# Causal attention on one core: masks taken off TensorE, small steps taken off VectorE

## The reference

```python
# 16 heads of 8 dimensions, 2 sequences of 2048, in chunks of 64 queries
scores = jnp.einsum('bhqd,bhkd->bhqk', qc, k) * scale
causal_mask = k_pos[None, :] > q_pos[:, None]
scores = jnp.where(causal_mask[None, None], -jnp.inf, scores)
m = jnp.max(scores, axis=-1, keepdims=True)
m = jnp.where(jnp.isinf(m), jnp.zeros_like(m), m)
p = jax.nn.softmax(scores - m, axis=-1)
oc = jnp.einsum('bhqk,bhkd->bhqd', p, v)
```

## Time and profile before

| | |
|---|---|
| median of three runs | 1788.74 us |
| profiled execution | 1792.63 us |
| its span | 1790.9 us |
| busy, TensorE / VectorE / ScalarE / GpSimd | 86% / 77% / 53% / 34% |
| L599, maxima: busy, idle before | 695.2 us, 64.8 us |
| L646, exponentials: busy, idle before | 607.1 us, 176.7 us |
| L687 and L695, masks: busy | 113.7 us, 115.3 us |

### The profile page before, as it was taken

How to read it: one execution, slowest core, us unless ns; L and a number is a source line. 1 busy time by engine, 2 the same in 40 slices (tenths; PEclk the granted TensorE clock), 3 DMA queues, 4 the chain that set the end, 5 groups by cost and what they waited for, 6 DMA issues and landing times. The chain is left out here.

```text
span 1790.9 us, 42250 instructions
## 1 busy us (share of the span) xinstructions
PE 1547.5 (86%) x13730; PEld 1004.8 (56%) x13730; DVE 1382.2 (77%) x2613; ACT 956.4 (53%) x2331; POOL 607.1 (34%) x416
## 2 busy tenths in 40 slices
PE   4499998999999999999972984899999999996376
PEld 3233333333333333333352874899999999996265
DVE  6799998998998999899653334588888888886522
ACT  4258887887887788788831322344444444442121
POOL 4600000000000000000015240988888888871633
PEclk9679999999999999999986996899999999997588
DMA  3320110011100110011063303011111222215340
GB/s 110 107 66 30 32 32 26 25 32 33 32 21 30 32 32 25 25 32 32 14 191 100 105 26 100 13 48 47 47 47 47 47 47 47 47 35 157 121 119 25
DMA packets 89477, 97.80 MB, mean 55 GB/s; under 512 B 12557, under 2 KB 74122, under 8 KB 89297
## 3 DMA queue, kind: packets, MB, share of 16 engines
q1 hardware_dynamic: 84176, 83.27, 16.4%
q0 software_dynamic: 5120, 12.26, 2.0%
HBM read 40.91 MB, written 31.85 MB: 41 GB/s over the span
## 5 line engine op out<-in xcount | busy, mean ns | idle before, releaser
L599 DVE TENSOR_REDUCE chunk_max<-ps_max 128x1 f32<-128x512 f32 (+3 forms) x1280 | 695.2, 604 | 64.8 <-PE ps_max L695 54.8
L646 ACT ACTIVATE probs<-ps_s 128x512 f32<-128x512 f32 (+3 forms) x1280 | 607.1, 534 | 176.7 <-PE ps_s L687 149.1
L1484 POOL TENSOR_TENSOR lane_products<-L,q 128x1024 f32<-128x1024 f32 x176 | 411.5, 2375 | 119.5 <-POOLq L1290 48.8
L668 PE MATMUL ps_s<-Qs,Ks 50*128 50x512 bf16 (+3 forms) x1280 | 376.7, 354 | 32.8 <-issue 13.8
L678 PE MATMUL ps_max<-Ks,Qs 48*128 48x512 bf16 (+3 forms) x1280 | 385.7, 360 | 13.8 <-POOL Vp L535 10.2
L741 PE MATMUL ps_o<-probs,Vp 128*32 128x512 f32 (+3 forms) x2560 | 344.1, 563 | 3.4 <-ACT probs L646 0.4
L668 PEld LDWEIGHTS ps_s<-Qs,Ks 50*128 50x128 bf16 x1280 | 113.9, 93 | 386.0 <-DVE chunk_max L599 327.1
L563 POOL COPY Vp<-V 128x128 f32 (+1 forms) x32 | 9.5, 299 | 740.3 <-PE ps_o L741 740.3
L1537 DVE TENSOR_TENSOR weighted<-exp_scores,psV_s 128x2048 f32<-128x2048 f32 x88 | 197.0, 2280 | 0.0
L1630 PE MATMUL psZT<-ident,weighted 128*128 128x128 f32 x1408 | 167.2, 274 | 1.8 <-DVE weighted L1537 1.8
L1630 PEld LDWEIGHTS psZT<-ident,weighted 128*128 128x128 f32 x1408 | 158.0, 141 | 2.0 <-DVE weighted L1537 2.0
(11 more groups left out here) (212 smaller groups left out, 2131.4 us busy)
## 6 DMA issues: line engine op xcount, KB each, us to landing
m_w<-in_L_ffn_w_dram SPq DMA_DIRECT2D x24, 512.0 KB, 6.9
dispatched<-blank SPq DMA_DIRECT2D x32, 258.0 KB, 3.0
m_d<-dispatched SPq DMA_DIRECT2D x14, 516.0 KB
L<-q SPq DMA_DIRECT2D x16, 448.0 KB
Qs<-q_parts SPq DMA_DIRECT2D x192, 32.0 KB
Ks<-k_parts SPq DMA_DIRECT2D x192, 32.0 KB
L<-q SPq DMA_DIRECT2D x20, 192.0 KB
L<-q SPq DMA_DIRECT2D x28, 128.0 KB
```

The source lines that it names most:

```text
L599: nc.vector.tensor_reduce(out, scores[:, 0:w], axis=AX.X, op=ALU.max).then_inc(max_reduced, 1)
L646: nc.scalar.activation(dst, ps_s[(k + r) % R][:, q0:], ACT.Exp, scale=SCALE).then_inc(exp_done, 1)
L668: last = nc.tensor.matmul(ps_s[(k + r) % R][:, q0:], K[r][rows, kt * P:(kt + 1) * P], Q[r][rows, g * QW + q0:(g + 1) * QW], start=True, st ...
L1484: return nc.gpsimd.tensor_tensor(out[:, l].rearrange("p (j m) d -> p j m d", m=LA), c.L[ch][:, :, l * LW:(l + 1) * LW].unsqueeze(2).broadc ...
```

## The change

The masks leave TensorE on both sides.

- For the maxima, VectorE uses `tensor_tensor_reduce` on the diagonal steps: it adds a constant fp32 tile `later` (0 at a query's own and earlier keys, -1e30 at later ones), writes the sum back to PSUM, and gives the maximum as an accumulated output. That instruction carries no wait of its own. Where the step before is a plain reduce, that reduce waits for the scores of both steps; where it is diagonal too (and at step 0), the wait stands on an increment of a counter ahead of it.
- For the exponentials, nothing is masked before them; GpSimd sets the later keys to zero in `probs` with `affine_select` on 128x128, 16 times a section, and `products` waits for the masks of its batch as well.
- Splitting the negated maximum in bf16 parts moves to GpSimd, at two places in its queue: after the masks of batches 0 to 2, and at the end of the section.
- ScalarE copies the combined output to SBUF after step 18 (`take_combined`), VectorE takes the reciprocal after step 22 (`invert`), GpSimd multiplies (`normalise`), after the masks of batches 3 to 5.
- The constants change: one tile `later` in place of the four bf16 mask tiles, and a zero tile for the split.

```diff
+    TAKE, INVERT = 18, 22
+    DIAGONAL = [kt >= 4 * g for g, kt in STEPS]
+    MASKS = [sum(DIAGONAL[:4 * n + 4]) for n in range(NBATCH)]
...
+            def split_maxima(s, r, f):
+                half = neg_max_b[r][:, f]
+                pool.wait_ge(neg_max_done, s * 2 + (f + 1))
+                nc.gpsimd.tensor_tensor(half[:, 0, :], neg_max[r][:, f, :], no_max[:], ALU.add).then_inc(neg_max_split, 1)
+                pool.wait_ge(neg_max_split, s * 4 + (2 * f + 1))
+                nc.gpsimd.tensor_tensor(half[:, 1, :], neg_max[r][:, f, :], half[:, 0, :], ALU.subtract)\
+                  .then_inc(neg_max_split, 1)
+
+            def normalise(s, p):
+
+                pool.wait_ge(inv_done, s)
+                nc.gpsimd.tensor_tensor(c.A_out[:, :, bass.ds(s - 1, 1), :].rearrange("p i s d -> p i (s d)"),
+                                        raw[p][:, :, 0:HD], inv[p][:].unsqueeze(2).broadcast_to([P, NQ, HD]), ALU.mult)\
+                  .then_inc(normalised, 1)
+
+            def mask(s, batches):
+                for n in batches:
+                    for q in range(4):
+                        k = 4 * n + q
+                        if DIAGONAL[k]:
+                            g, kt = STEPS[k]
+                            block = (probs[:, n % 3 * 4 + q] if n else probs0[:, q])[:, (kt - 4 * g) * P:(kt - 4 * g + 1) * P]
+                            pool.wait_ge(exp_done, s * NS + (k + 1))
+                            pool.sem_inc(masks_due, 1)
+                            nc.gpsimd.affine_select(out=block, in_=block, compare_op=ALU.is_ge, fill=0.0, base=0,
+                                                    pattern=[[1, P]], channel_multiplier=-1).then_inc(masked, 1)
...
+                if exp:
+                    mask(s, range(0, 3))
+                if nxt:
+                    split_maxima(s + 1, (r + 1) % R, 0)
+                if exp:
+                    mask(s, range(3, 6))
+                if exp and not (isinstance(s, int) and s == 0):
+                    normalise(s, p)
+                if exp:
+                    mask(s, range(6, NBATCH))
+                if nxt:
+                    split_maxima(s + 1, (r + 1) % R, 1)
 
             sections(pool, section)
+            normalise(NH, NH % 2)
+            pool.wait_ge(normalised, NH + 2)
...
             def negate_maxima(s, r, f):
-                half = neg_max_b[r][:, f]
                 nc.vector.tensor_reduce(neg_max[r][:, f, :], chunk_max[r][:, f * NQ // 2:(f + 1) * NQ // 2, :],
-                                        axis=AX.X, op=ALU.max, negate=True).then_inc(neg_max_steps, 1)
-                dve.wait_ge(neg_max_steps, s * 6 + (3 * f + 1))
-                nc.vector.tensor_copy(half[:, 0, :], neg_max[r][:, f, :]).then_inc(neg_max_steps, 1)
-                dve.wait_ge(neg_max_steps, s * 6 + (3 * f + 2))
-                nc.vector.tensor_tensor(half[:, 1, :], neg_max[r][:, f, :], half[:, 0, :], ALU.subtract)\
-                  .then_inc(neg_max_steps, 1)
-
-            def normalise(s):
-
-                dve.wait_ge(combined, s * GP)
-                nc.vector.reciprocal(inv[:], comb3[:, :, HD]).then_inc(inv_done, 1)
-                dve.wait_ge(inv_done, s)
-                nc.vector.tensor_tensor(c.A_out[:, :, bass.ds(s - 1, 1), :].rearrange("p i s d -> p i (s d)"),
-                                        comb3[:, :, 0:HD], inv[:].unsqueeze(2).broadcast_to([P, NQ, HD]), ALU.mult)\
-                  .then_inc(misc_read, 1)
+                                        axis=AX.X, op=ALU.max, negate=True).then_inc(neg_max_done, 1)
+
+            def invert(p, read):
+
+                dve.wait_ge(misc_read, read + 1)
+                nc.vector.reciprocal(inv[p][:], raw[p][:, :, HD]).then_inc(inv_done, 1)
...
                 for k, (i, ck) in enumerate(MAXES if nxt else []):
-                    dve.wait_ge(max_scored, (s + 1) * NS + (k + 1))
                     scores, out = ps_max[(k + r1) % R], chunk_max[r1][:, i, ck:ck + 1]
                     w = QW if ck < i // 4 else (i % 4 + 1) * P
-                    nc.vector.tensor_reduce(out, scores[:, 0:w], axis=AX.X, op=ALU.max).then_inc(max_reduced, 1)
+                    if DIAGONAL[k]:
+
+                        if k == 0 or DIAGONAL[k - 1]:
+                            dve.wait_ge(max_scored, (s + 1) * NS + (k + 1))
+                            dve.sem_inc(diagonal_due, 1)
+                        nc.vector.tensor_tensor_reduce(scores[:, 0:w], scores[:, 0:w], c.later[:, QW - w:], 1.0,
+                                                       LEAST, ALU.add, ALU.max, out).then_inc(max_reduced, 1)
+                    else:
+                        dve.wait_ge(max_scored, (s + 1) * NS + (k + 2 if k + 1 < NS and DIAGONAL[k + 1] else k + 1))
+                        nc.vector.tensor_reduce(out, scores[:, 0:w], axis=AX.X, op=ALU.max).then_inc(max_reduced, 1)
                     if k == FIRST_MAXES - 1:
                         dve.wait_ge(max_reduced, (s + 1) * NS + (AHEAD + k + 1))
                         negate_maxima(s + 1, r1, 0)
-                    if k == COMBINE_LAST[1] + 1 and exp and not first:
-                        normalise(s)
+                    if k == INVERT and exp and not first:
+                        invert(p, reads(s, "comb"))
...
+            def take_combined(s, p):
+                act.wait_ge(combined, s * GP)
+                act.wait_ge(normalised, s)
+                nc.scalar.activation(raw[p][:], comb3, ACT.Copy).then_inc(misc_read, 1)
...
+                        if k == TAKE and not first:
+                            take_combined(s, p)
...
-                diagonal = kt >= 4 * g
-                last = nc.tensor.matmul(ps_s[(k + r) % R][:, q0:], K[r][rows, kt * P:(kt + 1) * P],
-                                        Q[r][rows, g * QW + q0:(g + 1) * QW], start=True, stop=not diagonal)
-                if not diagonal:
-                    last.then_inc(scored, 1)
+                nc.tensor.matmul(ps_s[(k + r) % R][:, q0:], K[r][rows, kt * P:(kt + 1) * P],
+                                 Q[r][rows, g * QW + q0:(g + 1) * QW], start=True, stop=True).then_inc(scored, 1)
...
+                nc.tensor.matmul(ps_max[(k + r) % R][:, 0:w], Q[r][rows, i * P:(i + 1) * P],
+                                 K[r][rows, ck * QW:ck * QW + w], start=True, stop=True).then_inc(max_scored, 1)
...
-                for half in range(2 if diagonal else 0):
-                    if exp:
-                        mask_scores(r, p, k, half)
-                    if nxt:
-                        mask_for_max(r1, 1 - p, k, half)
...
+                pe.wait_ge(masked, s * MASKS[-1] + MASKS[n])
...
-                pe.wait_ge(neg_max_steps, s * 6 + 3 * (f + 1))
+                pe.wait_ge(neg_max_split, s * 4 + 2 * (f + 1))
```

More of the change, by code:

```diff
@@ L148, in _ @@
         def _(pool):
-            for t, value in ((c.ident, 0.0), (c.ident_b, 0.0), (c.causal, 0.0), (c.select, 0.0),
+            for t, value in ((c.ident, 0.0), (c.ident_b, 0.0), (c.later, 0.0), (c.select, 0.0),
                              (ones, 1.0)):
@@ L155, in _ @@
                                         pattern=[[-1, P]], channel_multiplier=1).then_inc(made, 1)
[L157 to L171 removed]
+            nc.gpsimd.affine_select(out=c.later[:, -P:], in_=c.later[:, -P:], compare_op=ALU.is_ge, fill=MASKED, base=0,
+                                    pattern=[[-1, P]], channel_multiplier=1).then_inc(made, 1)
             for g in range(4):
[L174 removed]
+                pool.wait_ge(made, 8 + g)
                 nc.gpsimd.affine_select(out=c.select[:], in_=c.select[:], compare_op=ALU.not_equal, fill=1.0,
@@ L529, in _ @@
             n = 0
-            for t, value in [(t, 0.0) for t in Vp] + [(t, LEAST) for t in chunk_max] + [(probs0, 0.0), (ones_row, 1.0)]:
+            for t, value in [(t, 0.0) for t in Vp] + [(t, LEAST) for t in chunk_max] + [(probs0, 0.0), (ones_row, 1.0), (no_max, 0.0)]:
                 nc.gpsimd.memset(t[:], value).then_inc(made, 1)
```

57 lines of the change are left out of this document (13 added, 44 removed).

## The result

The changed kernel takes 1882.93 us (median of 4 runs, 1882.25 to 1883.17), the kernel before 1788.55 beside it: a ratio of 1.0531 [1.0518, 1.0544], 94.4 us slower. The profiled execution took 1883.01 us, its span is 1881.3, 90.4 longer than before.

What follows compares the result with a forecast made beforehand. Neither TensorE nor VectorE plainly bound the heads: VectorE's queue and the round through TensorE were nearly equal. +3.2 us a head, 31 heads +98, ends about +2: 1889 us against the median, range 1846 to 1940.

Steps and rivals of the forecast that it cites:

- The wait that moves: Six rounds a head: a plain maximum also waits for the next diagonal step's scores, behind products; 15.3 to 17.8 + 6x us.
- x: Extra time of a diagonal maximum's accumulated output on VectorE; taken as 0.10 us, bounds 0 to 0.19.
- The accumulated output: VectorE's 16 masked maxima a head: the stream itself costs no more than reduces; each adds only x, taken as 0.10 us.
- The split on GpSimd: Turn of the head: two tiny GpSimd operations with hand-overs, 0.54 us, on the path; round 3.11 + x us, before 2.41.
- The rest of the head: The other 9.15 us of a head: fewer masked steps against extra waits and a late VectorE; together -0.07 + 2x us.
- The ends and the sum: Opening maxima-only head under +1 us, last normalisation about +1, 31 heads +98; 1893 us profiled, 1889 against the median.
- What I cost at nothing: GpSimd's masks ready before the products, ScalarE's extra copy, GpSimd's loop restart, SP's queue and DMAs: no time added.
- VectorE's queue alone decides: Rival: the held reduce costs nothing and VectorE's savings count; -0.7 us a head, 1766 us; chance 0.09.
- The accumulated output is dear: Rival: each accumulated maximum on VectorE costs 0.29 us extra, 4.7 us a head, 1937 us; chance 0.08.
- The clock: Rival: longer gaps between products drop TensorE's clock to 0.50 inside heads, +78 us, 1967 us; chance 0.05.
- GpSimd is late: Rival: GpSimd's masks come 0.3 us late in every round, +3 us a head, 1982 us; chance 0.03.

Runs made afterwards that it cites:

- e1: The changed kernel with every maximum waiting only for its own scores, each diagonal one by its own wait; 1798.78 us, ratio 1.0056.
- e11: The changed kernel with only the six shared waits that reach over products undone, the other three kept; 1798.85 us, ratio 1.0048.
- e2: The kernel before with only the shared wait added: a plain reduce before a diagonal step waits for both steps' scores; 1875.70 us, ratio 1.0491.
- e3: The changed kernel with the products issued behind the scores of each group's fourth step instead of the third; 1837.14 us, ratio 1.0280.
- e7: The kernel before with the products issued behind the scores of each group's fourth step instead of the third; 1846.12 us, ratio 1.0346.
- e10: The kernel before with only the masks for the exponentials moved from TensorE to GpSimd, behind the exponentials; 1791.75 us, ratio 1.0021.
- e5: The kernel before with only the normalisation moved: ScalarE copies, VectorE takes the reciprocal, GpSimd multiplies; 1782.40 us, ratio 0.9966.
- e6: The changed kernel with own waits for every maximum and both splits of the negated maxima back on VectorE; 1799.19 us, ratio 1.0054.
- e9: The kernel before with only the maxima's masks moved to VectorE as accumulated maxima, each with its own wait; 1819.58 us, ratio 1.0172.
- e4: The changed kernel with both splits of the negated maxima back on VectorE, shared waits kept; 1889.98 us, ratio 1.0549.

## Why the prediction was right, point by point

**The wait that moves.** Right in place and size. For the six rounds, from S15, S19, S27, S31, S35 and S39, the formulas with x = 0.10 give 3.20, 2.91, 3.20, 3.02, 2.84 and 3.21; measured are 3.19, 2.89, 3.19, 3.00, 2.81 and 3.26. The parts of the round from S27 can be read off one by one. S27 to R26 is 0.46 (0.45 predicted), R26 to R27 0.61 (0.60), R27 to S30 0.80 (0.75 + x), S30 to the products 0.32 (0.31), and these to S31 1.00 (0.99). The sum is this near because two small misses cancel: x is 0.05 and not 0.10, and four of the other parts are 0.01 longer each. e1, e11, e2 and the pair e3 and e7 show the cause from four sides: 84 us go with it, only its six places count, it alone makes 87 us in the kernel before, and without the products between it costs nothing that can be seen.

**The accumulated output.** The bounds, 0 to 0.19, held. x was taken as 0.10 and is 0.05 to 0.06: the custom operation's successor starts 0.60 to 0.61 after it, as after a plain reduce, and only what needs the result comes later. 0.80 less 0.75 is 0.05; at the turn R39 to the negation is 0.38, against 0.29 + x + 0.04. The prediction's "both about 1.05 ns an element" doesn't come from its two rows by division (1223 / 1024 is 1.19, 683 / 512 is 1.33); it holds for what each further element adds: (683 - 291) / 384 is 1.02 for reduces, (692 - 298) / 384 is 1.03 for the masked maxima. The Trainium skill ("VectorE: DVE Perf Modes", section "Two Vector instructions with no wait between them") says that such an operation is two instructions, and the trace agrees: 512 reads of the accumulator of 141 ns. From this I took that x isn't nothing, and it isn't. But the read starts together with the next operation and takes none of VectorE's stream.

**The split on GpSimd.** 0.54 plus 0.07 were predicted from the end of the negation to the turn; it is 495.28 to 495.89, 0.61. GpSimd's two operations are 0.20 each, as taken. The round is 0.05 over the formula, mainly since turn to S3 is 1.17 instead of 1.08.

**The rest of the head.** -0.07 + 2x, with 0.10 +0.13, was predicted for the other four rounds; they went from 9.16 to 9.27, +0.11. That this is so near is luck: the round from S23 grew by 0.13 where 0.23 was predicted, and the other three lost 0.02 together where 0.10 was.

**The ends and the sum.** A head grew by 3.12 (3.2 predicted), 31 of them are 97. The span grew by 90.4, where the sum had 100. The terms that were off are the smallest ones: I took the four restarts at the loop's branch as unchanged and the ends as +2. Between GpSimd's copies the heads with a restart took 19.3 us more than steady ones before, in sum, and some 14 with the one behind each after. And the ends, +2 in the sum, came out at -1.8: the first score matmul with exponentials starts 1.1 us earlier (99.5 for 100.6), and the stretch behind the last one is 0.7 shorter (886.2 for 886.8). So 1889 was 6 us above the measured 1883; on the profiled execution's terms, 1893 against 1883.

**What I cost at nothing.** The masks on GpSimd were in time (0.9 us of waiting in all), SP's queue too. e10 found what I had missed: they push GpSimd's copy of V to the turn, beside VectorE's subtraction, which then takes 0.13 longer; the changed kernel doesn't pay it at the turn, because its split isn't on VectorE.

**The rivals.** *VectorE's queue alone decides* fell with e1: even with own waits the head is 24.95, not 23.8. Of the 1.34 us a head that it counted as saved, the normalisation gives 0.34 (e5) and the splits nothing (e6 against e1); TensorE's masks, taken off for the maxima, cost VectorE 0.74 (e9). The parts add up: e6, which has just e9's, e5's and e10's, measured 24.89, and 24.48 + 0.74 - 0.34 + 0.13 is 25.01. Without the 0.13, since the subtraction isn't slow in e6, it is 24.88. *The accumulated output is dear*: x is 0.05 to 0.06, not 0.29. *The clock*: inside steady heads it stayed at 1.00, and 0.98 in the window against 0.99 before is the branch alone, where it fell to 0.50 for 3 to 7 us in either kernel. It moves in e3, e7 and e4 instead: at two branches of e3 it is low for 24 and 17 us, at two of e7 for 10, and in e4 in the last section. *GpSimd is late*: no.

## What to carry to other kernels

When two waits are merged, look at what the engine that signals does between the two signals. If it is a long burst, the first waiter stands behind the burst, and two engines that worked side by side take turns: here 87 us of 1789 from a single wait. And a change of many parts is to be taken apart on the chip, since this one held a part that gains 6 us, and the profile after shows only the loss.

## What the runs showed of the hardware

An accumulated maximum on VectorE costs 0.05 to 0.06 us of delay to whoever needs it, and next to no place in the stream: its operation of 512 takes 692 ns against a plain reduce's 686, and the read of 141 ns runs beside the next one. Behind it a plain reduce starts at most some 20 ns later than behind a plain one of the same width. A subtraction of 128x8 on VectorE took 298 to 303 ns instead of 168 where GpSimd's copy of 128x128 had begun 7 to 12 ns ahead of it (20 times in e10); where the copy had begun some 190 ns ahead it took 166 to 168 (e6). It isn't the copy alone: once it took 281 ns, with a mask begun 27 ns ahead (e4), and the subtraction ended 9 to 16 ns after GpSimd's operation each time. TensorE's clock need not be low in the same stretches in every kernel: the last section ran at 0.50 in e4's profile and took 35.7 us, at 1.00 in the kernel after and took 21.9; e4's runs lie 22 us apart, with mean granted clocks of 0.921 and 0.934. And a stretch with nearly the same code, from the last attention scores to the end, took 880 to 887 us in different profiles, so differences of a few us in the total aren't an edit's.
